# First attention layer: denominators seven steps a hop with copies of their buffers, queries split first on GpSimd, zeros in parts

## The reference

```python
q = qt.reshape(B * N_HEAD * m, d, N).transpose(0, 2, 1)
k2 = kt.reshape(B * N_HEAD * m, d, N2)
attn = jax.nn.softmax(jnp.einsum('bnd,bdk->bnk', q, k2) / temperature, axis=2)
attn = (attn * pi.reshape(-1, 1, 1)).reshape(B * N_HEAD, m, N, N2).sum(1)
out = jnp.einsum('bnk,bvk->bnv', attn, vt)          # then w_out, scale and shift, + x
```

## Time and profile before

| | us |
|---|---|
| median of 3 runs | 4171.39 (4158.77 to 4173.08) |
| the profiled execution | 4206.81 |
| its span, first to last instruction | 4205.0 |
| TensorE busy in the span | 3908.7 (93%) |
| VectorE, ScalarE, GpSimd busy | 2741.2, 2395.2, 855.5 |
| mean granted TensorE clock | 0.869 of full speed |

### The profile page before, as it was taken

How to read it: one execution, slowest core, us unless ns; L and a number is a source line. 1 busy time by engine, 2 the same in 40 slices (tenths; PEclk the granted TensorE clock), 3 DMA queues, 4 the chain that set the end, 5 groups by cost and what they waited for, 6 DMA issues and landing times.

```text
span 4205.0 us, 68871 instructions
## 1 busy us (share of the span) xinstructions
PE 3908.7 (93%) x26906; PEld 1017.8 (24%) x26906; DVE 2741.2 (65%) x8284; ACT 2395.2 (57%) x2830; POOL 855.5 (20%) x911
## 2 busy tenths in 40 slices
PE   6886878898988889999999999999999999999998
PEld 2211111212122122222222222222222222222222
DVE  5554545666566567776677766677777677777771
ACT  3543444555555653666656666656666656666665
POOL 3222222322332251102211101211011210110000
PEclk6756666766676686999999999999999999999999
DMA  1389784000000021222232222222322232322220
GB/s 48 27 53 54 52 56 37 14 14 13 14 14 13 12 70 35 82 79 63 67 89 66 67 66 79 68 79 65 97 69 66 76 78 64 83 78 65 80 68 25
DMA packets 268044, 236.23 MB, mean 56 GB/s; under 512 B 222184, under 2 KB 225112, under 8 KB 267464
## 3 DMA queue, kind: packets, MB, share of 16 engines
q1 hardware_dynamic: 241544, 205.85, 25.6%
q0 software_dynamic: 26176, 25.98, 2.7%
HBM read 226.65 MB, written 27.19 MB: 60 GB/s over the span
## 4 chain that ended last, share of the span: by engine, by line
PE 78%; DMA 7%; DVE 6%; issue 5%; POOL 3%; ACT 1%; POOLq 0%; SPq 0%; ACTq 0%; DVEq 0%
PE P L654 24%; PE P L639 18%; PE P L607 15%; PE P L620 7%; DVE maxes L964 5%; PE P L596 5%; PE P L680 4%; DMA rwide<-d_rden 3%; DMA d_rden<-rden 3%; PE P L730 2%; POOL high L478 1%; PE P L707 1%; PE P L696 1%; DMA den<-d_den 1%; PE P L741 1%
## 5 line engine op out<-in xcount | busy, mean ns | idle before, releaser
L854 ACT ACTIVATE probs<-P 128x896 f32<-128x896 f32 (+1 forms) x2352 | 2117.1, 916 | 1588.8 <-PE P L639 975.6
L983 DVE CUSTOM_DVE_ANT_0 junk<-P,mstage 112x448 bf16<-112x448 f32 x3136 | 1773.7, 621 | 674.2 <-PE P L607 673.7
L654 PE MATMUL P<-probs,vals 128*17 128x448 f32 (+1 forms) x9408 | 1292.0, 625 | 11.4 <-ACT sums L929 11.3
L964 DVE TENSOR_REDUCE maxes<-P 128x1 f32<-128x392 f32 (+1 forms) x1600 | 796.5, 558 | 519.0 <-PE P L596 518.5
L639 PE MATMUL P<-bstage,flip 112*56 112x448 f16 x6272 | 889.6, 364 | 0.0
L607 PE MATMUL P<-keys,q_stack 48*112 48x448 f16 x3136 | 744.7, 401 | 8.0 <-DVE maxes L983 6.2
L620 PE MATMUL P<-q_two,keys 49*128 49x448 f16 x3136 | 644.1, 352 | 0.0
L596 PE MATMUL P<-keys,q_stack 24*128 24x392 f16 (+1 forms) x1600 | 489.4, 430 | 141.3 <-DVE maxes L964 124.2
L607 PEld LDWEIGHTS P<-keys,q_stack 48*112 48x112 f16 x3136 | 286.4, 124 | 889.0 <-DVE maxes L983 461.1
L478 POOL TENSOR_SCALAR high<-projected,cst 128x448 f16<-128x448 f32 x112 | 157.0, 1402 | 1445.3 <-ACT projected L863 1393.7
L639 PEld LDWEIGHTS P<-bstage,flip 112*56 112x56 f16 x6272 | 210.8, 105 | 575.3 <-issue 575.3
(11 more groups left out here) (121 smaller groups left out, 1462.3 us busy)
## 6 DMA issues: line engine op xcount, KB each, us to landing
mstage<-g_max SPq DMA_DIRECT2D x56, 1519.0 KB, 8.0
bstage<-g_bias SPq DMA_DIRECT2D x28, 1568.0 KB, 8.4
bstage<-g_bias SPq DMA_DIRECT2D x28, 1519.0 KB, 8.1
rwide<-d_rden POOLq DMA_DIRECT2D x84, 224.0 KB, 5.0
g_max<-t_bf SPq DMA_DIRECT2D x16, 673.8 KB
g_bias<-t_hi SPq DMA_DIRECT2D x8, 679.9 KB
g_bias<-t_lo SPq DMA_DIRECT2D x8, 679.9 KB
wg<-in_wg POOLq DMA_DIRECT2D x12, 386.0 KB, 3.4
```

Of the source, the lines that this page charges most:

```text
L654: last = mm(P[32 * h:32 * h + HD + 1, PV, 0:QB], table[0:kr, kt, h, :], probs[0:kr, s % 3, h, :], start=kt == 0, stop=kt == unit.tiles - 1 ...
L854: A(probs[0:kr, s % 3, 2 * p:2 * p + 2, :], P[0:kr, 2 * p:2 * p + 2, 0:QB], ACT.Exp).then_inc(exp_done, 1)
L964: V.tensor_reduce(out=maxes0[0:size, unit.i % 2, t, HALVES[r], c:c + 1], in_=P[0:size, bank_of(job), 0:HALF], op=ALU.max, axis=AX.X).then_ ...
L983: V.tensor_tensor_reduce(out=junk[:, PLAN.nth[job] % 4, :], in0=P[0:QT, bank_of(job), 0:QB], in1=bias, scale=1.0, scalar=-3.0e38, op0=ALU. ...
```

## The change

Only the order and the buffers change; the arithmetic is the same. A table `STAGES` gives each unit the steps of its hops. For units 0 to 35 each DMA has 7 steps before the next stage waits for it, so that the output projection stands 32 steps after the unit's end; units 36 to 41 come down to 12, and from unit 42 on it is 12, with 2 steps a DMA. To hold that many units in flight, there are six `sums` and two `rwide` in the still unused `keys[0]` for units 0 to 41, four copies of `d_den` and `d_rden`, two of `den` and `rden`, and two semaphores for each DMA. GpSimd does a step's `stack` before its `normalise`. Output weights are multiplied into tiles of their own (`wout`). Groups 2 to 7 load their weights without waiting for an output projection, and every group scales them seven steps after the load. `keys[0]` is cleared after unit 41, and both tables in seven parts, one a step.

```diff
+SLOW, SUMS0, RDEN = 42, 6, 4
+CLEARS = 7
...
+def stages(i):
...
+    gap = min(7, max(2, SLOW - i)) if i < FIRST1 else 2
+    before = STAGES[-1] if STAGES else {}
+    at = {"copied": BASE[i + 1] + 1}
+
+    def follow(stage, step):
+
+        at[stage] = max(step, before.get(stage, step))
+
+    follow("stored", at["copied"])
+    follow("loaded", at["stored"] + gap)
+    follow("inverted", at["loaded"] + gap)
+    follow("stored_back", at["inverted"] + 1)
+    follow("widened", max(at["stored_back"] + gap, before.get("projected", 0) - 4 * (gap > 2)))
+    follow("multiplied", at["widened"] + gap)
+    follow("projected", at["multiplied"] + 2)
+    return at
...
-            put(BASE[i + 1] + (10 if i >= FIRST1 else 9), "b", "o", i)
+            put(STAGES[i]["projected"], "b", "o", i)
...
+        early_sums = keys[0][:, :, :].rearrange("p a n -> p (a n)").bitcast(F32).rearrange("p (k n) -> p k n", n=QB)
...
-                G.tensor_scalar(wg[k][:, OW:OW + 128], wg[k][:, OW:OW + 128], pi[:, at:at + 1], None, ALU.mult)\
+                if group >= 2:
+                    pool.wait_ge(yproj, (group - 1) * ROWS8)
+                G.tensor_scalar(wout[k][:, :], wg[k][:, OW:OW + 128], pi[:, at:at + 1], None, ALU.mult)\
                     .then_inc(wout_ready, 1)
...
+                for j in at_stage("multiplied", s):
+                    pool.wait_ge(rden_in[j % 2], landed(j))
+                    G.tensor_tensor(rwide_of(j), sums_of(j), rwide_of(j), ALU.mult).then_inc(scaled_made, 1)
+                for j in at_stage("widened", s):
+                    pool.wait_ge(rden_out[j % 2], landed(j))
+                    if rwide_free(j) > 0:
+                        pool.wait_ge(yproj, rwide_free(j))
+                    pool.dma_start(rwide_of(j), d_rden[j % RDEN].unsqueeze(1).broadcast_to([4, 32, QB])).then_inc(rden_in[j % 2], 16)
...
             for s in range(-PRE, LAST + POST):
-                normalise(s)
                 for w in "ab":
                     for job in PLAN.jobs[s - 1, w] if s > -PRE else []:
                         if job[0] in "qk":
                             stack(job)
+                normalise(s)
...
-                if s == 5:
-                    clear_second(0)
+                for k, at in ((0, STAGES[SLOW - 1]["projected"] + 1), (1, BASE[FIRST1 + 1] + 9)):
+                    if at <= s <= at + CLEARS:
+                        clear_second(k, s - at)
...
                 for group in range(2, len(UNITS) // ROWS8):
-                    if s == BASE[(group - 1) * ROWS8 + 1] + 3:
-                        pool.wait_ge(yproj, (group - 1) * ROWS8)
+                    early_load = group < NB * GROUPS0
+                    at = BASE[(group - 1) * ROWS8] + 4 if early_load else STAGES[(group - 1) * ROWS8 - 1]["projected"] + 1
+                    if s == at:
+                        if early_load:
...
                         load_group(pool, group)
+                    if s == at + 7:
                         scale_weights(group)
-                        if not is_biased(group):
-                            weigh_output(group)
+                    if early_load and s == BASE[group * ROWS8] + 10:
+                        weigh_output(group)
...
-                for j in (j for j in range(len(UNITS)) if s == BASE[j + 1] + 4):
-                    dve.wait_ge(den_in, 16 * (j + 1))
-                    V.reciprocal(rden[:, :, :], den[:, :, :]).then_inc(rden_made, 1)
+                for j in at_stage("inverted", s):
+                    dve.wait_ge(den_in[j % 2], landed(j))
+                    if j >= 2:
+                        dve.wait_ge(rden_out[j % 2], landed(j - 2))
+                    V.reciprocal(rden[:, j % 2, :, :], den[:, j % 2, :, :]).then_inc(rden_made, 1)
```

More of the change, by code:

```diff
@@ L86, with at_stage @@
 HALVES = (2, 3, 0, 1)
+def stages(i):
[12 more added lines that the diff above has]
+    return at
+STAGES = []
+for unit in UNITS:
+    STAGES.append(stages(unit.i))
+def at_stage(stage, s):
+    return [i for i, steps in enumerate(STAGES) if steps[stage] == s]
 class Plan:
@@ L220, in build @@
         sums = [sb(f"sums{k}", [128, QB]) for k in range(2)]
-        den = sb("den", [QT, 4, TILES])
-        rden = sb("rden", [QT, 4, TILES])
+        den = sb("den", [QT, 2, 4, TILES])
+        rden = sb("rden", [QT, 2, 4, TILES])
+        wout = [sb(f"wout{k}", [128, 128]) for k in range(2)]
         rwide = sb("rwide", [128, QB])
@@ L449, in normalise @@
[L449 to L456, removed]
@@ new lines, in normalise @@
+                for j in at_stage("widened", s):
[3 more added lines that the diff above has]
+                    pool.dma_start(rwide_of(j), d_rden[j % RDEN].unsqueeze(1).broadcast_to([4, 32, QB])).then_inc(rden_in[j % 2], 16)
+                for j in at_stage("stored_back", s):
+                    pool.wait_ge(rden_made, j + 1)
+                    if j >= RDEN:
+                        pool.wait_ge(rden_in[j % 2], landed(j - RDEN))
+                    pool.dma_start(d_rden[j % RDEN].rearrange("s (p a) -> p s a", a=TILES), rden[:, j % 2, :, :])\
+                        .then_inc(rden_out[j % 2], 16)
@@ new lines, in normalise @@
+                for j in at_stage("loaded", s):
+                    pool.wait_ge(den_out[j % 2], landed(j))
+                    if j >= 2:
+                        pool.wait_ge(rden_made, j - 1)
+                    pool.dma_start(den[:, j % 2, :, :], d_den[j % RDEN].rearrange("s (p a) -> p s a", a=TILES))\
+                        .then_inc(den_in[j % 2], 16)
+                for j in at_stage("stored", s):
+                    pool.wait_ge(sums_made, j + 1)
+                    if j >= RDEN:
+                        pool.wait_ge(den_in[j % 2], landed(j - RDEN))
+                    pool.dma_start(d_den[j % RDEN], sums_of(j)[HD:128:32, :]).then_inc(den_out[j % 2], 16)
@@ L489, in stack, with clear_second @@
                 G.tensor_tensor(o, f, h, ALU.add).then_inc(stacked, 1)
[L491 to L496, removed]
+            def clear_second(k, c):
+                if c < CLEARS:
+                    if k == 0 and c == 0:
+                        pool.wait_ge(yproj, SLOW)
+                    part, slots = 28 * 128 // CLEARS, 28 // CLEARS
+                    G.memset(keys[k][:, :, c * part:(c + 1) * part], 0.0).then_inc(cleared, 1)
+                    G.memset(vals[k][:, c * slots:(c + 1) * slots, :, :], 0.0).then_inc(cleared, 1)
+                    return
+                pool.wait_ge(cleared, clears(k) - 2)
+                G.memset(vals[k][0:W, :, :, HD:HD + 1], 1.0).then_inc(cleared, 1)
                 G.memset(vals[k][64:64 + W, :, :, HD:HD + 1], 1.0).then_inc(cleared, 1)
[L498 removed]
+                pool.wait_ge(cleared, clears(k))
             def pool_source(b):
@@ L729, in project_out @@
                 free(job)
-                mm(P[:, bank_of(job), 0:QB], wg[unit.group % 2][:, OW:OW + 128], rwide[:, :], start=True, stop=True)\
+                mm(P[:, bank_of(job), 0:QB], wg[unit.group % 2][:, OW:OW + 128] if unit.biased else wout[unit.group % 2][:, :],
+                   rwide_of(j), start=True, stop=True)\
                     .then_inc(yproj, 1)
@@ L923, in _ @@
                         exponentials(s, p)
-                    if p == 0 and s - 1 in BASE[1:]:
-                        j = BASE.index(s - 1) - 1
+                    for j in at_stage("copied", s) if p == 0 else []:
                         act.wait_ge(pv_done, s - 1)
-                        if j >= 2:
+                        if SUMS0 <= j < SLOW:
+                            act.wait_ge(scaled_made, j - SUMS0 + 1)
+                        elif j >= SLOW + 2:
                             act.wait_ge(scaled_made, j - 1)
-                        A(sums[j % 2][:, :], P[:, PV, 0:QB], ACT.Copy).then_inc(sums_made, 1)
+                        A(sums_of(j), P[:, PV, 0:QB], ACT.Copy).then_inc(sums_made, 1)
                     beside(s, w)
```

45 lines of the change are left out of this document (24 added, 21 removed).

## The result

| | before | changed |
|---|---|---|
| median of 4 runs | 4171.99 us (4158.77 to 4173.08) | 4088.12 us (4029.88 to 4132.26) |
| profiled execution | 4206.81, clock 0.869 | 4045.66, clock 0.904 |

The ratio is 0.9685 with a 95% interval of 0.9639 to 0.9731. Ratios with an interval leave out runs over 1.5% above the fastest of their kernel, here two of four, which differ from the others only by a lower mean clock (0.873 and 0.874 against 0.904 and 0.909). So the ratio of the medians of all runs stands beside each: here 4088.1 / 4172.0 = 0.980. The change saves 84 us at the median. The forecast was 105, 4066, with 4005 to 4125 as its range; the median lies between two runs near 4040 and two near 4131.

A forecast was written before the change was run, and what follows sets the result against it. Waits for the denominators' DMAs, while SyncE spreads the bias tables, were taken to bound the first layer. 106.8 + 3 - 5 = 105 us saved; 4171.4 - 105 = 4066 us, range 4005 to 4125.

The forecast's parts named there:

- 19 units at 24.32 us are 462.1 us in place of 568.9: 106.8 us saved: Units 2 to 21, first layer: without DMA waits they run at the undisturbed units' rate, saving 106.8 us.
- so I take none: First layer: no gain or loss counted for how often the upper clock is granted.
- a second rise: First layer: the moved output projection could start another rise of the clock in a unit; no gain counted.
- ±47 us: First layer: margin kept for the clock, 1 us a unit either way on 47 units.
- B: Rival, units 2 to 49: clock stays up without DMA waits, 18.25 us a unit, 3779 us; chance 0.07.
- C: Rival, units 2 to 49: moving the output projection removes the clock's rise, 27.35 us a unit, 4207 us; chance 0.04.
- D: Rival, units 2 to 21: GpSimd's DMA queue carries no more than now, 30.4 us a unit, 4180 us; chance 0.06.
- E: Rival: about half the loss stays, by late overlapping landings or splits behind pooling and loads, 4118 us; chance 0.17.
- +3: Near the second layer: the extra step a hop against splits going first, a net gain of 3 us.
- the first units of the block: Where the block begins while the ring fills: 3 to 5 us of remains, taken against the gain.

The follow-up runs named there:

- b_crowd_later: The kernel before with one added wait, so SyncE spreads the bias tables only after 21 units' sums are made; median 4174.2 us, ratio 1.0028.
- a_loads_at_once: The changed kernel with groups 2 to 7 scaling their weights right behind the load, in the same step; median 4118.6 us, ratio of medians 0.990.
- a_again: The changed kernel run once more, unedited, for the spread of its times; median 4127.8 us, ratio 0.9779.
- a_out_mod2: The changed kernel with the output projection of units 0 to 35 five steps later, one step behind the query projection; median 4045.7 us, ratio 0.9583.

## Why the prediction was right, and where it was not

**What bounds it.** Right. The block of small packets made the stretch slow (b_crowd_later), through the denominators' hops. Units 2 to 21 lost their waits, and the landings did not get shorter.

**Which part carries it.** The hops: with two steps the median is back at the kernel before, with four the gain is whole. The seven steps of the change are more than it needs. Queries first alone is worth nothing in the kernel before; beside seven steps a hop and neighbouring projections, undoing it together with the zeros cost 106 us by the means (4157 to 4051), and the traces put that down to the order. The prediction gave it no term of its own. The split of loading and scaling is worth nothing that can be seen. The zeros' own cost is 13.4 us for the fourteen pieces of `keys`, in idle time of GpSimd.

**The term that was mis-sized** is "19 units at 24.32 us are 462.1 us in place of 568.9: 106.8 us saved". It took the undisturbed units, with their clock of 0.69, as what the block would be without waits. Such units took 23.01 us at 0.75 in one execution and 26.82 at 0.57 in another. What the changed kernel saves at equal clock is 77 us by the lines of one chip (4192 to 4115), and on the other chip 57 by a_loads_at_once (4171 to 4114), which lies on the changed kernel's line. So the term was 30 to 50 us too large.

**The clock, "so I take none".** It was two effects, and they nearly cancelled. Taking the waits away with the projection left beside a query projection is worth 151 us by the means on one chip (4202 to 4051): 78 at equal clock, and as much again through the clock. Moving the projection three steps away costs 73 of it. The sum is 78, just what is saved at equal clock. That the clock could be taken at nothing was luck, and what is missing from 105 is the term above. The reason I gave for a gain from the place, a second rise, was seen, but half of such rises last only 3.4 us. The ±47 us kept for the clock were somewhat narrow: the ten runs of the changed kernel spread from 4030 to 4160, and five of them lie above 4125.

**The rivals.** B asked whether the clock stays up once the waits are gone. The clock does answer to the waits: 0.876 with two steps a hop, 0.902 with four. The Trainium skill ("TensorE: Matmul & The Clock Gate", section "HAM oscillation — how this bites in real kernels") says that waits for DMAs put TensorE back to the lower clock; these two runs agree with it in sign. But no run came near 18.25 us a unit throughout; the best stretch of 28 units took 22.34 us at clock 0.81. C had the right sign: the projection's move costs clock, though less than the waits gave. D is out by the overlap. E is out by its mechanism and not by its size: the savings of 74 us (a_again's median) and 84 lie between its 53 and the 105, but no wait for a hop is left on TensorE.

**The other parts.** The last stretch before the second layer took 237.5 us against 233.7, so its +3 did not come; units 0 to 2 took 5.1 us more (173.15 against 168.08), and the second layer 4.4 less. No wait remained in the first units of the block.

## What to carry to other kernels

Give each hop of a small transfer so many steps that its wait no longer reaches the engine that bounds the kernel, and no more. Here four steps of 3.35 us did, though the slowest landing took 14.7 us and GpSimd still waited up to 9.8; two did not. Look at every engine that waits for it in order: closing it on GpSimd alone left it to VectorE. A price of an unstalled step holds only for the clock it was read at; where TensorE is nearly but not quite full, compare kernels at equal clock, take several executions, and try where the long f32 matmuls stand.

## What the runs showed of the hardware

- One kernel, one chip, no waits for DMAs: 4080 to 4160 us, with mean granted clock 0.892 to 0.865. The kernel before spreads from 4139 to 4203 over 25 runs, clock 0.890 to 0.871.
- The place of one f32 projection of 1.8 us at the lower clock, once in a unit of 24 us, moves the whole kernel by 1 to 2%: next to another 0.901, three steps away 0.877; in the kernel before 0.876 and 0.860, there in part with new waits.
- In a_out_mod2 the clock falls into a pattern that repeats with the group of seven units:

```profile
810.34:963.94 153.60, 133.26 (x870) 33.26 (x869) 107.06 (x223) 96.79 (x123) 52.96 (x63) 0.81 0.07 15
```

  seven units in 153.60 us, 21.94 each. Why neighbours keep the clock up longer than the same matmuls apart was not settled: no run here measured it by itself.
